# Second attention by head group, with a DRAM round trip per head group; value projections of the first attention spread over the cycles

## The reference, cut to what matters

```python
rel = clip(r[:, None] - r[None, :], -64, 64) + 64
a_q, a_k, a_v = Eq[rel], Ek[rel], Ev[rel]
logits = (q k^T + einsum('bhld,lmd->bhlm', q, a_k) + einsum('bhmd,lmd->bhlm', k, a_q) + sum_d a_q a_k) * scale
attn = softmax(logits, axis=-1)
out = attn v + einsum('bhlm,lmd->bhld', attn, a_v)
```

## Time and profile before

| | |
|---|---|
| median of 3 runs | 936.7 us (935.32 to 937.66) |
| time of the profiled execution | 937.31 us |
| its span | 935.5 us |
| TensorE busy | 797.7 us (85%) |
| VectorE busy | 634.5 us (68%) |
| ScalarE busy | 487.0 us (52%) |
| POOL busy | 478.0 us (51%) |
| mean granted TensorE clock | 0.933 |

### The profile page before, as it was taken

How to read it: one execution, slowest core, us unless ns; L and a number is a source line. 1 busy time by engine, 2 the same in 40 slices (tenths; PEclk the granted TensorE clock), 3 DMA queues, 4 the chain that set the end, 5 groups by cost and what they waited for, 6 DMA issues and landing times.

```text
span 935.5 us, 14835 instructions
## 1 busy us (share of the span) xinstructions
PE 797.7 (85%) x6274; PEld 594.7 (64%) x6274; DVE 634.5 (68%) x519; ACT 487.0 (52%) x653; POOL 478.0 (51%) x256
## 2 busy tenths in 40 slices
PE   5889999999999999999999999868785132839878
PEld 2556777777777777777777777646665132727557
DVE  5048888788887887887887888895330009384895
ACT  4348557567476476475575675643321038523261
POOL 0026876876877867867868768595310111112200
PEclk9979999999999999999999999988887666959999
DMA  7110110110110110100101101011489850001001
GB/s 269 42 45 4 43 46 2 46 47 1 46 46 2 46 46 1 46 23 24 47 1 46 46 1 46 1 46 47 189 229 261 189 142 1 21 26 46 1 1 46
DMA packets 30353, 52.71 MB, mean 56 GB/s; under 512 B 2384, under 2 KB 25296, under 8 KB 26576
## 3 DMA queue, kind: packets, MB, share of 16 engines
q1 hardware_dynamic: 30288, 51.77, 18.3%
HBM read 41.87 MB, written 9.90 MB: 55 GB/s over the span
## 4 chain that ended last, share of the span: by engine, by line
PE 72%; DVE 9%; ACT 6%; SPq 4%; DMA 4%; issue 3%; POOL 1%; ACTq 0%; DVEq 0%
PE ps L299 22%; PE ps L307 21%; PE ps L352 13%; PE ps L370 6%; SPq L190 4%; DMA rel_scratch<-blocks 3%; PE ps L315 3%; PE ps L381 1%; PE ps L290 1%; ACT s_buf L749 1%; PE ps L502 1%; ACT v_buf L627 1%; DVE blocks L1087 1%; DVE s_buf L1186 1%; DVE rmax L1184 1%
## 5 line engine op out<-in xcount | busy, mean ns | idle before, releaser
L870 POOL TENSOR_TENSOR s_buf<-s_buf,r_all 128x1024 f32<-128x1024 f32 x94 | 198.7, 2151 | 2.9 <-DVE r_all L1025 2.9
L635 ACT COPY s_buf<-ps 128x1024 f32<-128x1024 f32 x128 | 129.7, 1013 | 68.3 <-PE ps L352 68.3
L352 PE MATMUL ps<-q_blk,k_t 64*128 64x256 f32 x1024 | 147.7, 408 | 6.7 <-ACT s_buf L635 6.7
L983 DVE TENSOR_REDUCE extra<-s_buf 128x128 f32<-128x2048 f32 x48 | 109.4, 2280 | 42.3 <-ACT s_buf L635 42.3
L644 ACT ACTIVATE s_buf<-s_buf 128x1024 f32<-128x1024 f32 x128 | 135.7, 1063 | 4.6 <-DVE s_buf L1005 4.5
L352 PEld LDWEIGHTS ps<-q_blk,k_t 64*128 64x128 f32 x1024 | 89.3, 188 | 54.8 <-issue 38.6
L619 ACT ACTIVATE k_t<-ps,cols 128x512 f32<-128x512 f32 x64 | 44.0, 688 | 129.6 <-PE ps L299 129.6
L1005 DVE TENSOR_TENSOR s_buf<-s_buf,ps 128x2048 f32<-128x2048 f32 x48 | 106.9, 2283 | 0.5
L1012 DVE TENSOR_REDUCE ps<-s_buf 128x128 f32<-128x4096 f32 x16 | 70.8, 4428 | 45.3 <-ACT s_buf L644 45.3
L848 POOL TENSOR_TENSOR odd_lo<-raw,odd_hi 128x512 fp32r<-128x512 f32 x32 | 41.3, 1290 | 113.8 <-ACT odd_hi L612 113.8
L842 POOL TENSOR_TENSOR v_buf<-v_buf,extra 128x512 f32<-128x512 f32 x64 | 82.7, 1295 | 14.6 <-ACT v_buf L627 14.6
(11 more groups left out here) (178 smaller groups left out, 1384.2 us busy)
## 6 DMA issues: line engine op xcount, KB each, us to landing
raw<-in_ctxT SPq DMA_DIRECT2D x16, 1024.0 KB, 4.8
s_buf<-rel_scratch SPq DMA_DIRECT2D x64, 128.0 KB, 4.0
rel_scratch<-blocks SPq DMA_DIRECT2D x10, 810.0 KB, 7.7
raw<-in_Wk SPq DMA_DIRECT2D x2, 1024.0 KB, 5.4
raw<-in_Wq SPq DMA_DIRECT2D x2, 1024.0 KB, 6.1
raw<-in_Wv SPq DMA_DIRECT2D x2, 1024.0 KB, 4.9
extra<-in_EvRel SPq DMA_DIRECT2D x1, 2048.0 KB, 9.5
x_res<-in_x SPq DMA_DIRECT2D x1, 1024.0 KB, 5.5
```

Of the source, the lines that this page charges most:

```text
L352: last = mm(ps[:, 2 + half_rows, i * 2 * P:(i + 1) * 2 * P], k_t[rows, hg, b * P:(b + 1) * P], q_blk[rows, b * C + hg, :], start=True, sto ...
L635: copy(piece(t, p).rearrange("p e (u n) -> p (e u) n", u=2), ps[:, 2:4, :]).then_inc(s["s_evac"], 1)
L870: pool.tensor_tensor(part, part, spread(r_all, 4), ALU.mult).then_inc(s["attn_pool"], 1)
L983: nc.vector.tensor_reduce(m_ps if k == 0 else m_next[:, k % 2, :], over_pairs(t, 2 * k, 2), AX.XY, ALU.max).then_inc(s["max_done"], 1)
```

## The change

**First attention.** The cycles of the value projections are a list: at the last four cycles of each tile from cycle 4 on, and at 128 to 132, but for five free cycles (13, 15, 30, 38, 128). The first tile's are at 4 to 7, and from cycle 44 on a tile's are where they were; the last tile's are at 129 to 132. In the last tile VectorE multiplies five of eight pieces, not four, and POOL three; POOL adds the value biases ahead of splitting Wo1. The bias of the output projection is added to x by POOL at the start, not at the end. ScalarE casts Wk2 ahead of the output projection's input and Wq2 ahead of the second layer norm's transposes.

**Second attention.** Rows are taken in groups of 32 (a row and batch make the 128 rows of a product), one head group hg at a time, both sides: 16 rounds of two groups, each 8 products of 159 columns into banks 0 to 3, with half projections of the next keys or queries between. Key-side rounds are copied by VectorE, query-side ones by ScalarE, into six slots. A store writes 256 runs of 2544 bytes; one load for each head group and side reads 512 runs of 2420 bytes, a run holding the 4 heads with 31 columns between that nothing uses. The keys and queries lie with the batch innermost, so one head's rows are at every fourth element. Logits are made and added in psum by head group, the softmax follows by head group, all exps are wide, and its sums are VectorE's. Value projections lie between the logits; the transposed probabilities are written back over the logits. POOL's copies of the queries are gone; its clearing of `blocks` comes ahead of two weights.

```diff
-LB = 8
-MB = P // LB
+LB = 32
+LG = P // LB
 WIN = P + LB - 1
-ROUNDS = [(3 * r, min(3 * r + 3, MB)) for r in range(6)]
-NROUND = len(ROUNDS)
-SLOTS = 5
+ROWS = J * WIN
+RUN = ROWS - LB + 1
+PITCH = ROWS + LB + 4
+GROUP = P * PITCH - LB
+NROUND = 4 * C
+SLOTS = 6
...
+        FREE = (13, 15, 30, 38, 128)
+        v_cycles = [n for n in range(8 * T + 5) if (n % 8 >= 4 or n >= 8 * T) and n not in FREE]
+        k_cycles = [n for n in range(8 * T) if n % 8 < 4]
+        cycles = sorted(k_cycles + v_cycles)
+
         def k_step(t, i):
-            return i if t == 0 else 8 * t - 4 + i
+            return cycles.index(k_cycles[C * t + i])
 
         def v_step(t, b):
-            return min(8 * t + 8, 8 * T - 4) + b
+            return cycles.index(v_cycles[B * t + b])
+
+        def v_at(n):
+            return divmod(v_cycles.index(n), B) if n in v_cycles else None
...
         def dve_pieces(t):
-            return 2 if t < T - 1 else 4
+            return 2 if t < T - 1 else 5
...
+        k_lb = v_buf[:, 0].rearrange("p b n -> p (b n)").rearrange("p (h l b) -> p h l b", h=C, b=B)
+        q_lb = k_t[:, :, :].rearrange("p h (l b) -> p h l b", b=B)
+
+        def by_row(t):
+            return t.rearrange("p l b -> p b l")
...
+        scratch = nc.dram_tensor("rel_scratch", (2, C, LG * GROUP), F32, kind="Internal").ap()
+        ring = blocks[:, :].rearrange("p g j q -> p (g j q)")
+        flat = s_buf[:, :, :, :].rearrange("p n h q -> p (n h q)")
+
+        def staged(n):
+            base = n % SLOTS * 2 * ROWS
+            return ring[:, base:base + 2 * ROWS].rearrange("p (g j w) -> p g j w", g=2, j=J)
+
+        def rows_of(t):
+            return t.rearrange("p (b r) -> p b r", b=B)
+
+        def rk_part(u):
+            return rows_of(flat[:, u * B * ROWS:(u + 1) * B * ROWS])
+
+        def rq_part(u):
+            slot = u % 3
+            if slot == 2:
+                return rows_of(extra[:, 0:B * ROWS])
+            return rows_of(flat[:, (C + slot) * B * ROWS:(C + slot + 1) * B * ROWS])
+
+        def heads(t):
+            return t.rearrange("p b (j w) -> p b j w", j=J)[:, :, :, 0:P]
+
+        lg_all = flat[:, 0:G * ROWS].rearrange("p (u b j w) -> p u b j w", u=C, b=B, j=J)[:, :, :, :, 0:P]
+
+        def lg(u):
+            return flat[:, u * B * ROWS:(u + 1) * B * ROWS].rearrange("p (n w) -> p n w", w=WIN)[:, :, 0:P]
...
+                kind = n // 2 % 2
+                sp.wait_ge(s["rk_evac" if kind else "rq_evac"], n // 4 * 2 + n % 2 + 1)
+                first = (n // 4 + kind * C) * LG * GROUP + 2 * (n % 2) * GROUP
+                dst = bass.AP(scratch.tensor, first, [[PITCH, P], [GROUP, 2], [1, ROWS]])
+                load(dst, staged(n).rearrange("p g j w -> p g (j w)"), f"rel_out_{n % SLOTS}")
+
+            def rel_load(kind, u):
+
+                for n in (4 * u + 2 * kind, 4 * u + 2 * kind + 1):
+                    sp.wait_ge(s[f"rel_out_{n % SLOTS}"], 16 * (n // SLOTS + 1))
+                first = (u + kind * C) * LG * GROUP + LB - 1
+                rows = bass.AP(scratch.tensor, first, [[B * PITCH - 1, P], [PITCH, B], [1, RUN]])
+                dst = rk_part(u) if kind else rq_part(u)
+                load(dst[:, :, 0:RUN], rows, f"rk_in_{u}" if kind else f"rq_in_{u}")
...
+            for n in range(4):
+                rel_store(n)
+            for u in range(C):
+                if u == 3:
+                    sp.wait_ge(s["lg_psum"], 1)
+                rel_load(0, u)
+                if u < C - 1:
+                    rel_store(4 * u + 4)
+                    rel_store(4 * u + 5)
+                rel_load(1, u)
+                if u < C - 1:
+                    rel_store(4 * u + 6)
+                    rel_store(4 * u + 7)
+            weight_load(4)
+            sp.wait_ge(s["lg_psum"], 3)
             load(ev_rel, a["EvRel"], "ev_in")
...
+            def relative(n):
+
+                hg, kind, part = n // 4, n // 2 % 2, n % 2
+                rows_lb, table = (q_lb, 0) if kind else (k_lb, 1)
+                if n == 0:
+                    pe.wait_ge(s["x1_done"], B)
+                elif n % 4 in (1, 2):
+                    pe.wait_ge(s["rq_evac"], 2 * hg + n % 4)
+                else:
+                    pe.wait_ge(s["rk_evac"], 2 * ((n - 1) // 4) + (1 if n % 4 == 3 else 2))
+                if part == 0:
+                    pe.wait_ge(s["q2_evac" if kind else "kf_evac"], hg + 1)
+                for g in (2 * part, 2 * part + 1):
                     for j in range(J):
                         rows = slice(j * HD, (j + 1) * HD)
...
+                        group = rows_lb[rows, hg, g * LB:(g + 1) * LB, :].rearrange("p l b -> p (l b)")
+                        window = P - LB * (g + 1)
+                        last = mm(ps[:, j, g % 2 * WIN:(g % 2 + 1) * WIN], group, tab[rows, table, window:window + WIN],
+                                  start=True, stop=True, skip_group_check=True)
+                last.then_inc(s["rel_psum"], 1)
...
+            def logits(u):
+                pe.wait_ge(s[f"rq_in_{u}"], 16)
+                if u == 0:
+                    pe.wait_ge(s["kf_evac"], C)
+                    pe.wait_ge(s["q2_evac"], C)
+                else:
+                    pe.wait_ge(s["lg_done"], u)
                 for j in range(J):
                     for b in range(B):
...
+                        mm(ps[:, 4 + j, b * P:(b + 1) * P], heads(rq_part(u))[:, b, j, :], ident[:],
                            start=b == 0, stop=False, is_transpose=True, skip_group_check=True)
                 for b in range(B):
                     for j in range(J):
                         rows = slice(j * HD, (j + 1) * HD)
...
+                        last = mm(ps[:, 4 + j, b * P:(b + 1) * P], q_lb[rows, u, :, b], k_lb[rows, u, :, b],
...
+                pe.wait_ge(s["exp2"], u + 1)
+                if u < 2:
+                    pe.wait_ge(s["v2_evac"], u + 1)
+                else:
+                    pe.wait_ge(s["lg_done"], C)
+                if u in (1, 3):
+                    pe.wait_ge(s["at_done"], B * u)
+                for b in range(B):
+                    for j in range(J):
+                        last = nc.tensor.transpose(ps[:, base + b, j * P:(j + 1) * P], lg_all[:, u, b, j, :], ident[:])
+                    last.then_inc(s["at_psum"], 1)
+
+            for k in range(2):
+                keys2(0, k)
+            for k in range(2):
+                queries2(0, k)
+            for hg in range(1, C):
+                for k in range(2):
+                    relative(4 * hg - 4 + k)
+                    keys2(hg, k)
+                for k in range(2):
+                    relative(4 * hg - 2 + k)
+                    queries2(hg, k)
+            relative(12)
+            logits(0)
+            for n in range(13, 16):
+                relative(n)
+            logits(1)
+            values2(0, 0)
+            logits(2)
+            attention_t(0)
+            logits(3)
+            values2(1, 0)
+            attention_t(1)
+            attention_t(2)
+            values2(2, 0)
+            values2(3, 1)
+            attention_t(3)
...
+            weight_hi(1)
             for b in range(B):
                 act.wait_ge(s["av_done"], 8 * (T - 1) + 4 + b + 1)
                 split_hi(b, 4 + b)
-            weight_hi(1)
...
+            keys2(0)
+            queries2(0)
+            for hg in range(1, C):
+                keys2(hg)
+                relative(4 * hg - 2)
+                relative(4 * hg - 1)
+                queries2(hg)
             weight_hi(3)
...
+            relative(14)
+            relative(15)
             exp2(0)
+            values2(0, 0)
             exp2(1)
+            at_copy(0)
             exp2(2)
...
+            values2(1, 0)
             at_copy(1)
             exp2(3)
             at_copy(2)
+            values2(2, 0)
+            values2(3, 1)
             at_copy(3)
+            weight_hi(4)
             for b in range(B):
                 act.wait_ge(s["av2"], b + 1)
                 copy(k_t[:, b, :], ps[:, b, :]).then_inc(s["ot2_evac"], 1)
+            weight_hi(5)
...
             pool.wait_ge(s["ln_done"], B)
             pool.wait_ge(s["bo_in"], 16)
             bo = bo_all.rearrange("p (o e) -> p o e", o=1).broadcast_to([P, B, D])
             pool.tensor_tensor(x_res[:], x_res[:], bo, ALU.add).then_inc(s["xb_done"], 1)
+            for t in range(T):
+                subtract(t)
+                between(t)
+                if t == T - 1:
+                    weight_lo(0)
+                normalise(t)
+
             for n in range(1, 4):
                 weight_lo(n)
-            for hg in range(C):
-                pool.wait_ge(s["q2_evac"], hg + 1)
-                pool.tensor_copy(from_natural(k_t[:, hg, :]),
-                                 q_perm[:, :, hg * B:(hg + 1) * B, :].rearrange("p u b e -> p b u e")).then_inc(s["q_nat"], 1)
+            pool.wait_ge(s["sub2"], C)
+            for slot in range(SLOTS):
```

(51 more changed lines are left out.)

272 lines of the change are left out of this document (74 added, 198 removed).

## The result

The changed kernel takes 879.32 us (median of 4, 877.37 to 880.67), the kernel before, timed beside it, 937.12: the ratio is 0.9386, 95% interval 0.9367 to 0.9406. The forecast was 871, with a range of 857 to 888. So 57.8 us came where 65.9 were summed. The profiled execution took 880.67 with a span of 878.9, 56.6 less than before's 935.5.

What follows compares the result with a forecast made beforehand. TensorE was taken to bound the first attention, and the order of two DRAM round trips the second. Savings of 59.4 + 4.7 + 1.75 = 65.9 from 937.3 give 871.4, less 0.6: 871 us, range 857 to 888.

Steps and rivals of the forecast that it cites:

- The second attention: From the first key projection to the value terms: 88.9 us against 148.3, so 59.4 us less.
- the strided price: Second attention's content matmuls, reading every fourth float: 2.7 us where they took 1.2, adding 1.5 us on the last logits.
- 8.9: Second attention, production of relative terms: 8.9 us per head group, from matmuls, psum copies and 0.1 us per round.
- the DMA engines are the bound: Second attention: a head group needs 13.8 us of DMA in 8.9 us of production, so the queue is never empty.
- 6.7 us each: Second attention's loads of relative terms: the upper end of their price, at 184 GB/s as for 512-byte rows.
- the first rival: Second attention's loads at the 512-byte price, each 3.3 us more, 23 us in all: 894 us; chance 0.08.
- following both engines' waits through cycles 12 to 16 gives 2.8 for the two: First attention: free cycles 13 and 15, where ScalarE is full, together save 2.8 us.
- cycles 4 to 7: First attention: value projections fill TensorE's idle time, 16.1 us for 11.4 + 1.2 including the low clock's cost: +3.5 us.
- Without the value copies between, the last total ends at 624.3: First attention's tail: the last softmax total ends at 624.3 us and r at 625.6, where r was at 627.2.
- The tail: End of the first attention: the output projection starts at 635.3 us, where it was 637.1, a gain of 1.75 us.
- Wq2's cast ahead of the splits lie under TensorE's 11.1 us: Ahead of the second attention: this cast and the bias add moved to the start cost nothing.
- the part ahead of the second attention: First attention and its tail, up to the first key projection: 4.7 and 1.75 us, together 6.45 us less.

Runs made afterwards that it cites:

- experiment 7: The changed kernel with six of its eight loads of relative terms reading two of four batches, 6.2 MB in place of 9.9; 879.37 us.
- Experiments 6 and 10: 6: changed kernel, each load of relative terms split into four with 512-byte runs, 879.0 us; 10: kernel before, 32 query-side reads joined into 8, 937.33 us.
- experiment 2: The changed kernel with free cycles 6, 7, 30, 38, 128 in place of 13, 15, 30, 38, 128; 874.35 us.
- experiment 3: The changed kernel with ScalarE's copies of the last tile's value projections 2 and 3 put one or two exps later; 876.02 us.
- experiment 1: The changed kernel with VectorE's one softplus instruction put behind the four low-part splits; 876.44 us.
- experiment 4: The changed kernel with the transposed probabilities written at a pitch of 128 floats per head in place of 159; 881.7 us.
- experiment 5: The changed second attention alone, with the first attention's cycles, pieces, biases and casts as in the kernel before; 877.82 us.

## Why the prediction was right, and where its sum was off

**The second attention** was right as a mechanism and in size: 58.25 us less for 59.4. The head groups make a pipeline, TensorE fills the round trips, and the last key-side load's landing (66.0 for 63.6) with the 24.0 us behind it (25.3) set the end. The adds measured 1.55 us a pair (1.5 forecast), the copies 1.22 (1.25), the content products 2.26 for four heads (2.7 with the strided price, 1.2 without). The head groups came 9.67 us apart and not 8.9. Each round waits for the copy of the one before:

```profile
680.97 0.58 PEld L456 LDWEIGHTS ps<-tab,v_buf 32*128 32x128 f32 x16 [0.52 <-DVE blocks L1125]
683.46 0.58 PEld L456 LDWEIGHTS ps<-tab,k_t 32*128 32x128 f32 x16 [0.51 <-DVE blocks L1125]
685.80 0.58 PEld L456 LDWEIGHTS ps<-tab,k_t 32*128 32x128 f32 x16 [0.36 <-ACT blocks L765]
688.14 0.58 PEld L456 LDWEIGHTS ps<-tab,v_buf 32*128 32x128 f32 x16 [0.36 <-ACT blocks L765]
```

A round with VectorE's copy takes 2.49 us, one with ScalarE's 2.34, where 2.36 and 2.11 were summed. The copies are as priced. But a copy starts 0.89 us behind the start of its round, and the next round starts 0.06 (VectorE) or 0.23 (ScalarE) behind the copy's end, where 0.86 us was summed for the two together. ScalarE's copies of the projections take 1.08 us for 0.59, as they write at every fourth float. The forecast had the layout's cost on TensorE's reading alone. That cost it little: these copies lie under the rounds, and the one wait of TensorE for them in this stretch is 0.51 us ahead of the first logits.

**"the DMA engines are the bound"** is right as what ends the last wait and wrong as what could be won: with 3.7 of 9.9 MB not loaded 1.35 us are gained in the stretch and none in the time (experiment 7). The rate was 392 GB/s over 690 to 722 where 367 was taken. A term that is the largest of several nearly equal ones looks like the only one in a sum that follows one chain.

**"6.7 us each" for loads in 512-byte runs**, the upper end and the first rival, had a wrong ground: 184 GB/s was read off as the price of the run's length. Experiments 6 and 10 show that neither the length alone nor the issues make it.

**The step that failed most** is "following both engines' waits through cycles 12 to 16 gives 2.8 for the two". It gave a loss of 0.36. The free cycles fell where ScalarE is full (it has no pause from 80.05 to 91.4 us), TensorE idled 2.67 and 1.99 us in a piece for the score's copy, and the clock fell (0.63 over 88.2 to 92.8 us): the next products took 1.97 and 1.91 us for 1.20 and 1.07. The clock was counted at cycles 4 to 7, where the change removes such a stretch, and not where the change makes one. Placed at 6 and 7, where ScalarE has room, the same two free cycles are worth 5.0 us by the times and 4.1 by the trace (experiment 2).

**"Without the value copies between, the last total ends at 624.3"** failed: the list of cycles takes the value projections only as far as 132, and two of the copies still stand in ScalarE's order ahead of the last exps, behind a burst of attend pieces on TensorE. The last total ended at 628.0. The tail came 1.58 us later where 1.75 earlier was forecast, and 3.3 us come back when the two copies are moved (experiment 3).

**"Wq2's cast ahead of the splits lie under TensorE's 11.1 us"** is right for ScalarE's cast. What was not followed is who waits for it: POOL's split of that weight, which so came to lie beside VectorE's small softplus instruction, and that one stands ahead of the four splits. Price 2.41 us; moving it brings back 2.7 by the trace, 2.9 by the medians (experiment 1).

**Unforeseen and for the change**: the value terms, 2.6 us, by the pitch of the probabilities (experiment 4). **Not of the change**: 2.48 us of the start in the profiled execution, 2.09 of them by the low clock there. That the time fell within the range owes something to luck: the part ahead of the second attention was forecast at 6.45 us less, and experiment 5 shows no gain from it, and the value terms gave 2.6 that nobody counted. The steps add up: forecast less seen is 1.15 in the second attention and 10.65 ahead of it, and 2.6 come back, 9.2 in all, the 65.9 forecast against 56.6 of the span.

## What to carry to other kernels

When a cast or a load is moved, follow it to whoever waits for it, and look at what then runs beside that: one 16-column instruction with its inputs in SBUF cost as much as the POOL instruction beside it. Free slots are worth their whole length only where every engine of the cycle has room; elsewhere TensorE idles and pays again in its clock. And when a resource is busy all through a stretch, take some of its work away before calling it the bound: here the next engine's order stood 1 us behind it.

## What was not expected of the hardware

- A VectorE instruction of 128x16 with all inputs in SBUF took 4.50 us beside a POOL instruction of 4.68; VectorE's 128x512 splits, with one input in psum, kept their 0.69 us beside the same POOL instruction.
- Products of 64 columns read at a pitch of 512 bytes took 10.5 us for 128 of them, at 636 bytes 8.1: 82 against 63 ns each.
- A ScalarE copy of 128x512 into every fourth float took 1.08 us, into contiguous ones 0.60; products whose two operands lie at every fourth float took 2.26 us for 16, contiguous ones 1.17. The Trainium skill (SBUF — State Buffer, Door 1: The DMA port swizzle) says that each access that crosses to a new 16-byte line pays a penalty. The trace agrees in kind, with the two pairs of times here.
- A 512-byte packet took its engine 31.0 ns in one layout, mixed with long stores, and 44.9 in another; a 2420-byte one 105 ns. The engines were full in all three.
- The query projection of the start took 13.97 us in three of the twelve profiled executions and 15.67 to 16.48 in the others. In the three its products are 0.43 us apart from the first one on; in the others they are 0.85 apart until 19.0 to 20.6 us, where the trace's clock rows begin.
